# One PSUM bank moved from the maxima to the scores in a decoder layer: three and two in place of two and three

## The reference, cut to what matters

```python
x = x + attn(layernorm(x), wq, wk, wv, wo)            # 32 heads of 16, causal
C_q, C_kv = layernorm(x) @ Wq_d, ctx @ Wkv_d          # ctx: (16, 1500, 512), C_kv: (16, 1500, 32)
scores = einsum('bnhl,bkl->bhnk', (C_q @ W_qk).reshape(b, n, 16, 32), C_kv) / sqrt(32)
x = x + einsum('bhnk,bkhd->bnhd', softmax(scores), (C_kv @ Wv_u).reshape(b, 1500, 16, 32))
x = x + ffn(layernorm(x))                             # kernel, bias, low-rank A and B
```

## Time and profile before

| | |
|---|---|
| time, median of 3 runs | 644.15 us (641.67 to 647.26) |
| the profiled execution: its own time | 645.84 us |
| the profiled execution: its span | 644.0 us |
| granted TensorE clock over the span | 0.968 |
| busy: TensorE, VectorE, GpSimd, ScalarE | 584.1, 432.5, 412.7, 302.1 us |
| DMA over the span | 77.4 MB moved, mean 120 GB/s |

### The profile page before, as it was taken

How to read it: one execution, slowest core, us unless ns; L and a number is a source line. 1 busy time by engine, 2 the same in 40 slices (tenths; PEclk the granted TensorE clock), 3 DMA queues, 4 the chain that set the end, 5 groups by cost and what they waited for, 6 DMA issues and landing times.

```text
span 644.0 us, 11508 instructions
## 1 busy us (share of the span) xinstructions
PE 584.1 (91%) x4164; PEld 315.5 (49%) x4164; DVE 432.5 (67%) x715; ACT 302.1 (47%) x642; POOL 412.7 (64%) x385
## 2 busy tenths in 40 slices
PE   7889797998999899999999899998999899988887
PEld 7436353455446354545446355455446355434445
DVE  2737964678757967778747957678757967656632
ACT  1421434537444555437444555437444555464460
POOL 5002166598758887598758887588758887789000
PEclk9997788899999999999999999999999999999899
DMA  9959511651048110751039110761039110200000
GB/s 320 409 107 348 208 36 24 251 206 35 12 120 317 59 45 22 268 204 39 9 108 336 52 45 22 253 219 32 16 93 334 68 45 23 64 19 0 24 2 15
DMA packets 31578, 77.40 MB, mean 120 GB/s; under 512 B 11297, under 2 KB 24961, under 8 KB 29218
## 3 DMA queue, kind: packets, MB, share of 16 engines
q1 hardware_dynamic: 30854, 75.27, 34.9%
q10 hardware_dynamic: 668, 1.40, 0.6%
HBM read 58.92 MB, written 2.88 MB: 96 GB/s over the span
## 4 chain that ended last, share of the span: by engine, by line
PE 58%; DVE 19%; ACT 6%; POOL 4%; SPq 4%; issue 4%; DMA 4%; ACTq 0%; POOLq 0%; DVEq 0%
PE st_ps L711 11%; PE mx_ps L754 9%; PE pv_ps L726 8%; PE mi_ps L496 4%; PE mi_ps L490 4%; DVE mx_p L1143 4%; POOL acc L1214 3%; PE mi_ps L503 3%; DVE p L1066 2%; PE mi_ps L586 2%; SPq L402 2%; DMA ctx_sb<-in_ctx_t 2%; DVE xn L1018 2%; PE mi_ps L590 2%; DVE p L1107 2%
## 5 line engine op out<-in xcount | busy, mean ns | idle before, releaser
L1214 POOL TENSOR_TENSOR acc<-acc,p_ring 125x448 f32<-125x448 f32 x290 | 348.0, 1200 | 65.4 <-ACT p_ring L941 25.8
L1143 DVE TENSOR_REDUCE mx_p<-mx_ps 128x1 f32<-128x500 f32 x336 | 210.0, 669 | 98.9 <-PE mx_ps L754 97.9
L941 ACT ACTIVATE p_ring<-st_ps 125x448 f32<-125x448 f32 x372 | 183.4, 544 | 151.6 <-PE st_ps L711 139.7
L711 PE MATMUL st_ps<-q_st,c_st 98*125 98x448 f32 x372 | 146.3, 432 | 9.8 <-ACT p_ring L941 8.6
L754 PE MATMUL mx_ps<-c_st,q_st 96*128 96x500 f32 x336 | 142.1, 457 | 12.2 <-DVE mx_p L1143 5.1
L711 PEld LDWEIGHTS st_ps<-q_st,c_st 98*125 98x125 f32 x372 | 65.3, 190 | 99.3 <-ACT p_ring L941 79.9
L726 PE MATMUL pv_ps<-p_ring,c_nat 125*32 125x448 f32 x768 | 94.5, 564 | 1.9 <-ACT ox L840 1.0
L754 PEld LDWEIGHTS mx_ps<-c_st,q_st 96*128 96x128 f32 x336 | 63.6, 197 | 43.7 <-DVE mx_p L1143 17.6
L1222 POOL TENSOR_TENSOR rstd<-mv,eps_col 128x1 f32<-128x1 f32 x24 | 4.6, 190 | 117.1 <-DVE mv L1014 116.6
L503 PE MATMUL mi_ps<-ctx_sb,wkv_sb 128*32 128x375 f32 x480 | 46.8, 511 | 5.5 <-DVE p L1066 5.5
L1214 POOL TENSOR_TENSOR acc<-p_ring 125x448 f32<-125x448 f32 x29 | 35.6, 1226 | 19.2 <-ACT p_ring L941 19.2
(11 more groups left out here) (137 smaller groups left out, 677.9 us busy)
## 6 DMA issues: line engine op xcount, KB each, us to landing
ctx_sb<-in_ctx_t SPq DMA_DIRECT2D x16, 3000.0 KB, 11.6
c_st<-ct_hl SPq DMA_DIRECT2D x192, 46.9 KB, 2.3
q_st<-q_hl SPq DMA_DIRECT2D x90, 56.0 KB, 2.0
x_sb<-in_x SPq DMA_DIRECT2D x8, 256.0 KB, 2.8
out_y<-x3n SPq DMA_DIRECT2D x16, 112.0 KB
wq_sb<-in_wq SPq DMA_DIRECT2D x2, 512.0 KB, 6.4
kern_sb<-in_lora_a SPq DMA_DIRECT2D x1, 1024.0 KB, 14.2
wo_sb<-in_wo SPq DMA_DIRECT2D x1, 1024.0 KB, 17.6
```

What stands on the lines that cost most here:

```text
L711: mm(st_bank(unit)[0:KC, 0:HALF], c_st[:, b % 4, t * KT + k * KC:t * KT + (k + 1) * KC], q_st[:, b // 2 % 2, b % 2, half * HALF:(half + 1) ...
L941: act.activation(p_ring[:, unit % PR, :], st_bank(unit)[0:KC, 0:HALF], ACT.Exp, scale=float(L) ** -0.5).then_inc(exp_done, 1)
L1143: ve.tensor_reduce(mx_p[:, p:p + 1], mx_ps[unit % MXB][:, 0:KP], AX.X, ALU.max).then_inc(red_done, 1)
L1214: po.tensor_tensor(dst, first, p_ring[:, unit % PR, :].rearrange("p (h s) -> p h s", s=S), ALU.add).then_inc(acc_done, 1)
```

## The change

`STB` becomes 3 and `MXB` 2. Unit n now waits for the exponential of unit n-3, and piece n for the reduction of piece n-2. The last batch has four score banks before and after; they are now three of `st_ps` and one of `mx_ps`, so the wait for the last reduction moves from its third unit to its fourth. In the prologue the first `V` and the fillers move to score banks, and a wait for the copy of `V` is put ahead of the first low-rank products.

```diff
@@ -50,8 +50,8 @@
 EPS = 1e-5
 NEG = -1e30
 PR = 8
-STB = 2
-MXB = 3
+STB = 3
+MXB = 2
 GROUPS = 2 * KG
 ADDS = 4 * KG - 1
 
@@ -326,7 +326,7 @@
             if n == 0 and name in ("Ah", "A"):
                 return mx_ps[MXB - 1]
             if n == 0 and name == "V":
-                return mx_ps[MXB - 2]
+                return st_ps[1]
             b = BANK[name]
             return mi_ps[b[n % 2] if isinstance(b, tuple) else b]
 
@@ -504,7 +504,7 @@
                                   ctx_sb[:, slot, c, t * KT:(t + 1) * KT], start=(c == 0), stop=(c == CH - 1))
                 return last
 
-            def fill(count, bank_=mx_ps[MXB - 1]):
+            def fill(count, bank_=st_ps[0]):
 
                 for _ in range(count):
                     mm(bank_[:, 0:128], ident[:, :], ident[:, :], start=True, stop=True)
@@ -702,9 +702,9 @@
                 if g == 0 and t == 0:
                     pe.wait_ge(m_in[b % 2], 32 * (b // 2 + 1))
 
-                if b == B - 1 and g == 0 and t == 2:
+                if b == B - 1 and g == 0 and t == STB:
                     pe.wait_ge(red_done, B * PIECES)
-                if b == B - 1 and (g or t > 1):
+                if b == B - 1 and (g or t >= STB):
                     pe.wait_ge(exp_done, unit - 3)
                 elif unit >= STB:
                     pe.wait_ge(exp_done, unit - STB + 1)
@@ -785,6 +785,7 @@
             pe.wait_ge(s1_sb, 4)
             step("CT", 0)
             fill(6, mx_ps[0])
+            pe.wait_ge(v_sb, 4)
             lora_factors(0, 2)
             for name in ("P0", "P1"):
                 step(name, 0)
```

## The result

The changed kernel takes 702.65 us (median of 4 runs, 700.27 to 703.01), the kernel before, beside it on the same chip, 644.6 (641.67 to 647.26): a ratio of 1.0901, interval 1.0861 to 1.0941. I had forecast 682 and a range of 660 to 700. The direction was right, the size not: 58 us more where I had 38, and 2.65 us beyond the range. The profiled execution of after took 700.27 us with a span of 698.5, 54.4 more than the one of before. The ratios in this document are worked out from all runs of both kernels and not from the two medians, so they can differ by some 0.4% from the medians' ratio; one run that the record marks as slow, e10's at 673.18, is not in them.

A forecast was written before the change was run, and what follows sets the result against it. TensorE standing still in its in-order queue was taken as the bound. 5.2 us a body, 31 for bodies 1 to 6, plus 3.3 and 3.8 at the ends made 38 on 644.15: 682 us, range 660 to 700.

The forecast's parts named there:

- the three bursts: Pieces 3 to 5, 14 to 16, 27 to 29: each third piece waits for the first's reduction, 0.70 each, 2.1 us a body.
- piece 38: Ahead of `H`, it waits for reduction 36 behind VectorE's third normalisation statistics; cost 1.2 us a body.
- piece 41: Near the body's end, it waits for reduction 39 behind `H` and `N2` on VectorE; cost 1.0 to 1.1 us.
- the clock: Rival: added TensorE stops bring dips of the granted clock, 10 to 20 us on top, 692 to 702; chance 0.18.
- piece 8: After the first burst, it waits for reduction 6 behind VectorE's split of the latents and `N0`; cost 0.8 us a body.
- The third score bank: Removes a unit's wait in the sixth group, but TensorE then waits at later pieces; 0 a body, -0.5 at the other end.
- Pieces 18 to 20: Piece 20 would wait for reduction 18, but `Ah` behind it waits for VectorE anyway; cost 0, other end 0.6 us.
- Body 0: First body: pieces 7 and 8 some 1.0, two bursts 1.4, piece 23 0.9; together 3.3 us.
- Body 7: Last body: first half 1.3, then GpSimd's pace hides the rest up to piece 41, 2.5; together 3.8 us.
- the one stop of the sixth group: TensorE idles 0.92 us before the third of four units, waiting for exponentials; taken as all 8.6 us of units' matmul waits.

The follow-up runs named there:

- e10: e6 with GpSimd's wait for VectorE's split of the latents kept in bodies 1 to 6 alone: 667.93 us, ratio 1.0322.
- e8: Changed kernel, TensorE multiplying identity matrices ahead of the waits of pieces 8 and 38 in bodies 1 to 6, into the next unit's score bank: 694.07 us.
- e6: Changed kernel with e2's wait, the third piece of each of three bursts behind the next step, and piece 38 behind `H`: 668.98 us, ratio 1.041.
- e2: Changed kernel, but GpSimd waits for VectorE's split of the latents before its first addition in bodies 1 to 7: 686.13 us, ratio 1.0681.
- e9: Kernel before, three maxima banks, but piece 5 of bodies 1 to 6 waits for the reduction two before it: 655.66 us, ratio 1.0157.
- e7: e1 with TensorE multiplying identity matrices into the idle bank ahead of the waits of pieces 8 and 38 in bodies 1 to 6: 702.3 us.
- e1: Changed kernel with score banks back to two, so two of each kind, the eighth idle up to the last batch: 718.35 us, ratio 1.1135.
- e12: Kernel before, with identity products at three places where TensorE stops in body 0: 644.68 us, ratio 0.999.
- e3: Changed kernel with piece 5 (and its like in body 0) behind the latents' second half on TensorE: 691.86 us, ratio 1.0746.

## Why the prediction was right and wrong

Right were the bound (TensorE standing still in its own queue), the direction, the three bursts, piece 38, and piece 41 once the clock is out (e8). e6 shows that the terms of the bursts are real and separate: moved, they are gone.

**The step that failed first is piece 8, sized at 0.8.** I moved VectorE's work along by 0.70 as a block and let every instruction keep its duration, and I wrote that nothing on GpSimd gets in front, by its 16 us of idle time. But the split stood right ahead of GpSimd's additions, and GpSimd's start hangs on the statistics of the first normalisation, which did not move. Late by 0.6, the split ran into them: 0.34 and 0.55 us became 1.10 and 1.45, and piece 8, which with two banks needs a reduction behind split and normalisation, came 2.5 late. e2 takes the collision away (and shortens the normalisation too) and piece 8 costs less than 0.1; between e2 and e8, bodies without slow clock differ by 2.4 us; e9 makes the collision without a change of banks. Over six bodies the term was 1.7 each too small, some 10 us; part of it was caught up directly behind and in bodies 1 and 4, where the kernel before had its own slow clock, so that bodies 1 to 6 come to 36.4 us in e8 where I had 31.

The Trainium skill ("SBUF — State Buffer", Who interferes with whom) has the rule: VectorE's casts and scalar forms, where they run in a two-port mode, contend with GpSimd for a port pair, which one of the two holds for its whole instruction; an operation with two SBUF inputs contends with GpSimd's reads; and a reduction never contends. The trace agrees for each kind: the cast, the subtraction and the normalisation grow beside additions, to less than an addition's 1.15 and their own time together, while reductions keep 0.64 to 0.68. That it is this port was not measured; that GpSimd's running is the cause was, by e2.

**The second is the clock, put at 0.18 as a rival.** My argument against it was that the bodies of before have one stop of 0.92 us each, and of bodies 2 to 6 only one a dip. But the change adds stops that are longer (2.25) or stand near others (piece 38's 1.10 between those of `T2`, `CQ` and `H`), and nearly every body got one or two slow stretches: 41.0 us at half clock in bodies 1 to 6 for 9.5. e7 and e8 show it as cause and not as company, since filling two waits removes them. In bodies 1 to 6 it cost 8.3 us (481.1 against 472.8) for 37.6 us of slow time that the fillings removed. That is less than the 18.8 that half of it would be, as slow stretches replaced waits that would have come, piece 41's above all. What the rival priced, 10 to 20 us, is a little above that; its chance was too low.

**The smaller terms.** The third score bank took 0.64 a body and lost 0.5 of it again at pieces 23 to 25, by the steps I gave. With only two maxima banks its absence costs more, 0.8 to 0.9 and then the clock (e1, e7): neither bank could be spared on top. Pieces 18 to 20 cost 0.3, between my ends. Body 0 was 5.8 for 3.3: by piece 9 TensorE is 1.6 late (I had 1.0), by piece 20 4.8, of which 2.2 are back before piece 23, whose 4.0 shrink to 1.7 by piece 25, where I had 0.9. Body 7 was 4.0 for 3.8, and that is luck: it is 2.8 late before piece 38, where I had 1.3, the rest comes at piece 38 (3.2 late) and not at 41, and of that 2.2 are back at piece 39.

**Two readings.** I took the units' 8.6 us of waiting for the one stop of the sixth group, once in a body; that stop is 5.5 of it, in bodies 1 to 6, and 2.05 stand at the end of body 0. And the ends of my terms give 674 to 687, not the 672 to 692 that I gave the forecast for itself. Neither bears on the miss.

The profiled executions' 54.4 us divide into 36.4 and 8.3 in bodies 1 to 6 and 5.8 and 4.0 at the ends. All but the split between 36.4 and 8.3, which is e8's, is read off the same two traces, so that the parts add up proves nothing. The medians lie 58 apart; the last 3.6 are that before's profiled execution was 1.2 above its median and after's 2.4 below.

Open stay why e10's runs fall in two groups of different granted clock, why TensorE is 4.8 late by piece 20 of body 0, how much body 7 loses to GpSimd's wait when the rest is moved too, and why e12's gain in one execution doesn't show in the median.

## What to carry to other kernels

When a step comes later, look at what runs on the other engines at its new time: a duration read from a row holds only beside the company that it had there. A stop that is added to the engine on the path costs its length and then perhaps the clock; where there is idle PSUM, work without use ahead of the wait tells the two apart in one run. And of two kinds of banks in one queue, both can be short at once: price the bank that is given away at each place where its exchange is one deep.

## What the hardware showed beyond that

The same cast of 128x375 took 0.34 us with no addition of GpSimd beside it and 1.10 to 1.31 beside one, the subtraction 0.55 and up to 1.54, the normalisation of 128x512 0.54 and 1.37. The long ones stand in the kernel before too, where they hurt nobody. Which side pays hung on who began first: in the kernel before the subtraction kept its 0.55 and the addition took 1.54 for 1.15; in e3, with the addition 0.03 us ahead (206.62 and 206.65), the subtraction took 1.53 and the addition 1.14. And TensorE, given 22 matmuls more in a body (e7 against e1, body 2), was busy for 1.9 us less.
